# Attention and routing kernel: the row maxima turned by VectorE and sent by SyncE, a third unit loaded early, and a norm folded into the logits

## The reference, cut to what matters

```python
# x: (4, 1024, 256), fp32
x = x + _layernorm(attention(_layernorm(x)))
x = x + _layernorm(ffn(_layernorm(x)))

# attention: 16 heads of 16, relative positions (DeBERTa: content-to-position and position-to-content)
scores = einsum('bhqd,bhkd->bhqk', q, k) / scale
scores = scores + (c2p + p2c) / scale        # both gathered by the bucket of q - k
probs = softmax(scores)
out = layernorm((probs @ v) @ Wo + bo + hidden_states, 1e-7) * ln_scale + ln_bias

# ffn: router, then the one expert that it picks
routing_logits = x @ Wr + br                 # 8 experts, x is the normalised input
indices = argmax(softmax(routing_logits))
for i in range(8):
    h = relu((x * mask_i) @ W1[i] + b1[i]);  out = out + h @ W2[i] + b2[i]
```

## Time and profile before

| | us |
|---|---|
| median of 3 runs | 1785.49 |
| lowest, highest | 1784.4, 1792.77 |
| the profiled execution | 1794.4 |
| its span, first to last instruction | 1792.3 |

### The profile page before, as it was taken

How to read it: one execution, slowest core, us unless ns; L and a number is a source line. 1 busy time by engine, 2 the same in 40 slices (tenths; PEclk the granted TensorE clock), 3 DMA queues, 4 the chain that set the end, 5 groups by cost and what they waited for, 6 DMA issues and landing times. The chain is left out here.

```text
span 1792.3 us, 41887 instructions
## 1 busy us (share of the span) xinstructions
PE 1615.2 (90%) x13688; PEld 1147.8 (64%) x13688; DVE 1364.4 (76%) x3868; ACT 1145.8 (64%) x2764; POOL 1030.9 (58%) x1264
## 2 busy tenths in 40 slices
PE   7963799999999999999999999999977866999997
PEld 4531566666666666666666666666634646999996
DVE  4753798999998999898899998999956754555553
ACT  6852587877877888878777878787754631222221
POOL 0003776777776777777777777777814622333332
PEclk9985899999999999999999999999997857999998
DMA  4986788878888788788888887888608616666762
GB/s 136 332 284 221 246 278 275 273 264 267 269 280 275 261 275 279 256 272 286 269 265 267 268 274 260 273 264 281 211 25 220 190 65 197 194 193 198 206 202 57
DMA packets 292450, 421.65 MB, mean 235 GB/s; under 512 B 35382, under 2 KB 233804, under 8 KB 292139
## 3 DMA queue, kind: packets, MB, share of 16 engines
q1 hardware_dynamic: 271640, 378.99, 65.2%
q10 hardware_dynamic: 16851, 30.67, 5.6%
q0 software_dynamic: 3744, 9.31, 1.4%
HBM read 241.39 MB, written 177.79 MB: 234 GB/s over the span
## 5 line engine op out<-in xcount | busy, mean ns | idle before, releaser
L934 ACT ACTIVATE t_probsT<-t_flip 128x512 f32<-128x512 f32 x1024 | 603.2, 615 | 192.3 <-PE t_flip L791 103.3
L851 DVE TENSOR_REDUCE t_most<-t_scores 128x1 f32<-128x640 f32 (+1 forms) x512 | 435.7, 851 | 120.1 <-PE t_scores L775 119.4
L997 POOL TENSOR_TENSOR t_near<-t_near,masks 128x384 f32<-128x384 f32 (+1 forms) x128 | 146.5, 1144 | 275.5 <-DMA t_near<-skew_d 274.8
L861 DVE CUSTOM_DVE_ANT_0 t_band<-t_scores,t_near,t_most 128x384 f32<-128x384 f32 (+1 forms) x512 | 297.0, 580 | 0.5 <-DVE t_most L851 0.2
L872 DVE TENSOR_SCALAR_CACHE_REDUCE t_band<-t_band,t_top 128x384 f32<-128x384 f32 (+1 forms) x512 | 291.2, 569 | 0.0
L926 ACT COPY t_table<-t_table_ps 128x388 f32<-128x388 f32 x502 | 251.2, 500 | 54.1 <-PE t_table_ps L747 50.9
L812 PE MATMUL t_sum_ps<-t_probsT,vals 128*32 128x256 f32 x4096 | 274.3, 385 | 0.3 <-ACT t_probsT L934 0.3
L1013 POOL TENSOR_TENSOR t_near<-t_near,masks 128x768 f32<-128x768 f32 (+1 forms) x128 | 268.6, 2098 | 0.0
L775 PE MATMUL t_scores<-masks,t_near 128*128 128x128 f32 x1408 | 244.8, 278 | 19.6 <-POOLq L1016 18.8
L798 PE MATMUL t_flip<-masks,t_band 128*128 128x128 f32 x1408 | 258.1, 274 | 0.0
L768 PE MATMUL t_scores<-afters,quests 105*128 105x256 bf16 (+3 forms) x1024 | 244.3, 288 | 3.8 <-DVE t_top L861 3.6
(11 more groups left out here) (212 smaller groups left out, 2572.4 us busy)
## 6 DMA issues: line engine op xcount, KB each, us to landing
skew_d<-t_table SPq DMA_DIRECT2D x128, 1024.0 KB, 11.3
t_near<-skew_d SPq DMA_DIRECT2D x128, 640.0 KB, 8.0
t_near<-skew_d SPq DMA_DIRECT2D x128, 384.0 KB, 7.4
e_w<-in_L_ffn_W_dram ACTq DMA_DIRECT2D x39, 512.0 KB
e_w<-in_L_ffn_W_dram SPq DMA_DIRECT2D x39, 512.0 KB
split_d<-p_part SPq DMA_DIRECT2D x32, 384.0 KB, 3.3
afters<-split_d SPq DMA_DIRECT2D x128, 96.0 KB
quests<-split_d SPq DMA_DIRECT2D x128, 96.0 KB
```

Source lines behind the costliest of these rows:

```text
L851: nc.vector.tensor_reduce(most[:, c:c + 1], out[:, wide:S], AX.X, ALU.max).then_inc(far_seen, 1)
L861: nc.vector.tensor_tensor_reduce(band[n % 2][:, t, 0:wide], out[:, 0:wide], near[n % 2][:, 0, t, at:at + wide], 1.0, most[:, c:c + 1], ALU ...
L934: nc.scalar.activation(probsT[s % 4][:, half * 512:(half + 1) * 512], flip_ps[half][:, :], ACT.Exp, scale=SCALE).then_inc(expd, 1)
```

## The change

- `attend`, the maxima: the three parts lie in a tile of four (the fourth zero), VectorE turns them itself in four blocks of 32 by 32 (`turn_top`, after `look(s)` at s = 8n + 9), waiting for GpSimd's split. TensorE's L820 and ScalarE's L946 and L948 go, with the waits around them and the bf16 identity. SyncE issues the transfer (`send_top(u - 1)`), between the near read of unit u + 1 and the loads of unit u + 4.
- `attend`, loads: unit 2 is loaded in `project`, at its step 6 (`EARLY` = 3), the first `load_far` moves to step 7, and `Wo` is loaded at u = 12 into a tile kept for `mix`.
- `mix`: TensorE's program starts when `Wo` (landed long ago) and the bias rows are there. The third norm is not applied to the rows: their sum `x2` is turned and multiplied by `Wr` as it is, and the norm's factor and shift are put into the logits for all tokens at once behind the loop. ScalarE applies two norms instead of three in a step, and the loop of VectorE and ScalarE has 18 full steps instead of 20. The first two norms' statistics go to PSUM. `b1` is loaded by rows and turned by TensorE, not by a transfer of single elements.

```diff
-EARLY = 2
+EARLY = 3
@@ project, sync
                 if s == 6:
+                    hats.load_unit(sp, split_d, 2)
+                if s == 7:
                     hats.load_far(sp, far_d, 0)
@@ attend, sync
+            def send_top(n):
+                sp.wait_ge(top_turned, n + 1)
+                sp.dma_start(quest[n % BUFS][MROW:ROWS, :], topT[n % 2][0:PARTS * QT, :]).then_inc(top_in[n % BUFS], 16)
+
             for u in range(-2, N + 3):
...
                 if u == -2:
                     skew_read(0, 0)
+                if 0 <= u - 1 < N:
+                    send_top(u - 1)
                 if EARLY <= u + 4 < N:
                     load_unit(u + 4)
...
+                if u == 12:
+                    sp.dma_start(wo[:, :, :], Wo.rearrange("(k p) n -> p k n", p=P)).then_inc(wo_in, 16)
@@ attend, tensor
-                if x >= AHEAD and (x - AHEAD) % QT == 2:
-                    pe.wait_ge(top_kept, (x - AHEAD) // QT)
...
-            def turn_top(n):
-                pe.wait_ge(split_made, 5 * (n + 1))
-                pe.wait_ge(table_kept, by_act(min(n * QT + QT + AHEAD + 2, TS) - 1))
-                nc.tensor.matmul(table_ps[0:PARTS * QT, 0, 0:P],
-                                 top_part[n % 2][:, :, :].rearrange("p a t -> p (a t)"), ident16[:, :],
-                                 start=True, stop=True).then_inc(top_turned, 1)
@@ attend, vector
+            def turn_top(n):
+                dve.wait_ge(split_made, 5 * (n + 1))
+                if n < 2:
+                    dve.wait_ge(parts_set, 2)
+                if n >= 2:
+                    dve.wait_ge(top_in[(n - 2) % BUFS], 16 * ((n - 2) // BUFS + 1))
+                for a in range(4):
+                    last = nc.vector.transpose(topT[n % 2][:, 32 * a:32 * a + 32],
+                                               top_part[n % 2][32 * a:32 * a + 32, :, :].rearrange("p a t -> p (a t)"))
+                last.then_inc(top_turned, 1)
...
                 look(s)
+                if s > QT and s % QT == 1:
+                    turn_top(s // QT - 1)
@@ attend, scalar
-            def keep_top(n):
-                act.wait_ge(top_turned, n + 1)
...
-                nc.scalar.copy(topT[n % 2][:, :], table_ps[0:PARTS * QT, 0, 0:P]).then_inc(top_kept, 1)
-                act.wait_ge(top_kept, n + 1)
-                nc.scalar.dma_start(quest[n % BUFS][MROW:ROWS, :], topT[n % 2][:, :]).then_inc(top_in[n % BUFS], 16)
@@ mix, sync
-            loads = [(wo[:, :, :], Wo.rearrange("(k p) n -> p k n", p=P)),
-                     (ls_b[:, :], row(ln_s, D)), (lb_b[:, :], row(ln_b, D)),
+            loads = [(ls_b[:, :], row(ln_s, D)), (lb_b[:, :], row(ln_b, D)),
...
-            for dst, src in [(b1_sb[:, :, :], b1.rearrange("e (c p) -> p e c", p=P)), (b2_sb[:, :], b2),
+            for dst, src in [(b1_rows[:, :], b1.rearrange("e (c p) -> (e c) p", p=P)), (b2_sb[:, :], b2),
@@ mix, vector
+            dve.wait_ge(row_norm, 4)
             dve.wait_ge(logit_made, NG)
             link(nc.vector.tensor_tensor(logits[:, :, :], logit_ps[:, 0:NT * E].rearrange("p (t e) -> p t e", e=E),
-                                         br_b[:, :].unsqueeze(1).to_broadcast([P, NT, E]), ALU.add))
+                                         row_inv[:, :].unsqueeze(2).to_broadcast([P, NT, E]), ALU.mult))
+            link(nc.vector.tensor_tensor(logits[:, :, :], logits[:, :, :], offset[:, :, :], ALU.add))
@@ mix, scalar
-                for i in range(lo, hi):
+                for i in range(lo, min(hi, 2)):
@@ mix, tensor
-                pe.wait_ge(norm_made[2], g + 1)
+                pe.wait_ge(x2_made, g + 1)
-            pe.wait_ge(loaded, 16 * 6)
+            pe.wait_ge(wo_in, 16)
             pe.wait_ge(bo_made, 7)
```

More of the change, by code:

```diff
@@ L130, in build @@
             spent = sem.spend()
-            attend(nc, sem, spent, masks, rows, hats, split_d, far_d, v_d, skew_d, ctx_d)
+            attend(nc, sem, spent, masks, rows, hats, split_d, far_d, v_d, skew_d, ctx_d, Wo, wo, wo_in)
         sem.take_back(spent)
@@ L567, in _, with attend @@
                 last.then_inc(far_made, 1)
-def attend(nc, sem, spent, masks, rows, hats, split_d, far_d, v_d, skew_d, ctx_d):
+def attend(nc, sem, spent, masks, rows, hats, split_d, far_d, v_d, skew_d, ctx_d, Wo, wo, wo_in):
     AHEAD = 2 * QT + QT // 2
@@ L1037, in _ @@
             nc.gpsimd.memset(before_rows[:, :], -1.0).then_inc(before_set, 1)
+            for i in range(2):
+                nc.gpsimd.memset(top_part[i][:, PARTS:4, :], 0.0).then_inc(parts_set, 1)
             pool.wait_ge(before_set, 1)
@@ L1241, in _ @@
                 dve.wait_ge(stats_made, norms_before[s + 1])
-                for i in range(lo, hi):
+                if hi > 2:
+                    g = s - 2 * LAG
+                    for t in range(G):
+                        last = nc.vector.bn_aggr(row_mv[:, g * G + t, :], stats[:, c, 2, t, :])
+                    last.then_inc(row_mv_made, 1)
+                if s >= NORMED:
+                    continue
+                for i in range(lo, min(hi, 2)):
                     for t in range(G):
@@ L1346, in keep_xf @@
                 nc.scalar.copy(xfT[g % 2][:, :, :], xf_ps[:, :, :]).then_inc(xfT_made, 1)
-            for s in range(STEPS):
+            for s in range(NORMED):
                 if s in W2_AT:
@@ L1360, in _ @@
                 if hi > 1:
-                    a = max(lo, 1)
-                    last = nc.scalar.activation(root[:, c, a:hi, :], mv[:, c, a:hi, :, 1], ACT.Sqrt, bias=eps[:, 1:2])
+                    last = nc.scalar.activation(root[:, c, 1, :], mv[:, c, 1, :, 1], ACT.Sqrt, bias=eps[:, 1:2])
                 last.then_inc(root_made, 1)
-                if s >= 2 * LAG + 1:
-                    keep_xf(s - 2 * LAG - 1)
+                if s >= TURN:
+                    keep_xf(s - TURN)
                 act.wait_ge(shift_made, s + 1)
-                for i in range(lo, hi):
+                for i in range(lo, min(hi, 2)):
                     g = s - LAG * i
-                    src, dst = ((y1, y4), (y4, y5), (x2, xf))[i]
+                    src, dst = ((y1, y4), (y4, y5))[i]
                     if i == 1 and g >= BUFS:
                         act.wait_ge(x2_made, g - BUFS + 1)
-                    if i == 2 and g >= BUFS:
-                        act.wait_ge(xf_turned, g - BUFS + 1)
                     for t in range(G):
@@ L1377, in _ @@
                     last.then_inc(norm_made[i], 1)
-            keep_xf(NG - 1)
+            for g in range(NORMED - TURN, NG):
+                keep_xf(g)
+            act.wait_ge(row_mv_made, NG)
+            nc.scalar.activation(row_root[:, :], row_mv[:, :, 1], ACT.Sqrt, bias=eps[:, 1:2]).then_inc(row_root_made, 1)
             act.wait_ge(const_made, 2)
@@ L1428, in constant_rows @@
                 last.then_inc(const_made, 1)
[L1430 removed]
+            pe.wait_ge(wo_in, 16)
             pe.wait_ge(bo_made, 7)
             project_out(0)
[L1433 removed]
+            for s in range(NG + TURN + 1):
                 if s + 1 < NG:
                     project_out(s + 1)
[L1436 removed]
+                if s == 2:
+                    pe.wait_ge(loaded, 16 * 5)
+                    pe.wait_ge(const_in, 48)
+                    nc.tensor.transpose(aside_ps[:, 0:E * KC], b1_rows[:, :], ident[0:E * KC, 0:E * KC])
+                    for k in range(2):
+                        last = nc.tensor.matmul(aside_ps[:, E * KC:E * KC + E], masks[:, 3, :], wr[:, k, :],
+                                                start=(k == 0), stop=(k == 1))
+                    last.then_inc(aside_made, 1)
+                g = s - TURN
                 if 0 <= g < NG:
```

85 lines of the change are left out of this document (51 added, 34 removed).

## The result

| | us |
|---|---|
| before, median of 4 runs on the same chip | 1787.93 (1784.4 to 1792.77) |
| after, median of 4 runs | 1916.89 (1912.85 to 1919.51) |
| ratio | 1.072, 95% interval 1.068 to 1.0755 |
| predicted | 1820, range 1755 to 1880 |

The account below looks back on a forecast made before the run. The prediction took the queue of transfers to bound attention. From this execution's 1794.4 us, +61 for late maxima, -7 for the third unit and -20 for mix gave 1828.4, less 8.9 to the median: 1820 us, range 1755 to 1880.

Parts of the forecast that it names:

- The loop over two units: Attention: two periods = 20.4 + one unit's compute + 0.3 us, so period 18.8 against 17.8, +61 us.
- The queue drains: Attention: later flips mean later loads, so old work ahead goes; last flip to near read's landing falls from 23.7 to 20.4 us.
- rival 2: Attention: the maxima land in time despite the near read ahead of them, no stall; 1758 us, chance 0.20.
- a unit's compute without the queue: Attention: VectorE's 16.1 us, plus 0.4 for the transposes and 0.4 for waits that stay, 16.9 us.
- rival 1: Attention: stalls cost clock (1845 to 1880 us) or the queue doesn't drain (1936 us); chance 0.15.
- the spread in attention: Forecast's own spread from compute 16.5 to 17.3 and drained loop 19.6 to 21.2 us: +27 to +104 us.
- VectorE's turning: Attention: four small transposes a unit, 0.3 to 0.6 us, taken 0.4; ready at some 700.3, before the near read's issue.
- Rival 3: Attention: VectorE's transposes wait for GpSimd's split and hold up all looks; around 1840 us, chance 0.07.
- The queue is the bound: Attention: the queue of transfers sets the 17.8 us unit, though its mean share is 0.82; some engines must be full.
- Rival 4: Attention: compute, not the queue, is the bound and freed time counts; -30 to -55, 1704 to 1730 us, chance 0.08.
- Third unit early: Loading unit 2 in `project` lets table writes go 3 us earlier; gain 0 to 9 us, taken 7.
- `mix`: After attention: start -4, `b1` -2, steps -9, tail -5 us; sum -20, between -8 and -30.

Follow-up runs that it names:

- The filled stall: Changed kernel with 20 more products ahead of the first flip of every second unit, results overwritten: 1864.2 us, ratio 1.0439.
- with the queue relieved: Kernel before with all but the maxima's part, table writes cut to a quarter from unit 2 on (tells of time only): 1736.43 us, ratio 0.9694.
- the rest alone: Kernel before with early unit 2, early `Wo` and the whole of `mix`, maxima as before: 1766.55 us, ratio 0.988.
- the two with both places moved: Changed kernel, maxima turned one look sooner, issued by ScalarE (1769.47 us) or by SyncE ahead of the near read (1767.64 us).
- spread loads: Operand loads reordered, slowest dimension 16 rows, not three: all but the maxima 1761.55 us; changed kernel 1872.53; turned sooner with ScalarE issuing 1772.79.

## Why the prediction was wrong in size

**What held.** The maxima land right behind the near read. The loop over two units is the one that was written down: two periods = the way from the loads to the landing, one unit's compute, and 0.3 us. With the values of the trace after, (21.1 + 19.53 + 0.3)/2 = 20.5; the stalls come 40.8 us apart (202.68 to 1344.49 in 28 times), so 20.4. The queue drains as said: the way is 21.1 us (713.09 to 734.19), near the 20.4 taken, far from 23.7.

The Trainium skill's page DMA: Bandwidth & Descriptors, section on queues, rings and completion order, says that a queue is consumed in ring order and that queues take turns. The traces agree with both halves: on one queue the two landings release their engines 0.15 us apart, and from ScalarE's queue or from ahead of the read the maxima come in about 5 us (medians of the units that wait: 5.3 and 4.9). Its remark that completion isn't in order of issue, rival 2 of the prediction, brought nothing here.

**The step that failed** is the term "a unit's compute without the queue", 16.9 us. It was taken at full clock. In the stalled unit it is 19.53 us: +1.3 us a unit of the 1.7 missing; the longer way, +0.7, gives the other 0.35. The cause was on the page: the earlier trace rows show a clock of 0.57 for 4 us behind a gap in TensorE's work, and the prediction made of it rival 1, at 0.15, with 0.4 to 0.9 us a period. Its price was too low as well: it counted "a few us at half clock", 0.4 to 0.9 us a period, where the 6.8 us behind this stall lose 3.0 us in every second unit, so 1.5 us a period (1.4 by the median of the stalls). The filled stall shows that this is cause and not company. With the clock kept, the same formula gives (21.3 + 16.7 + 0.3)/2 = 19.15 us (21.3: the loads of a unit at 687.87 to the landing at some 709.2), and its two units of 38.4 us bear that out; the mean is 19.3. The filled kernel is still 44 us above the forecast: some 33 of them are 0.54 us a unit of period (0.45 by the longer way), and most of the rest is the 7 us of the third unit, whose gain the first stall eats there too (first exponential at 203.5 us).

Two of the prediction's sums don't come out as it gives them. From its own bounds the spread in attention is +24 to +98, not +27 to +104, and its other two terms together give 8 to 39 us back, not 16 to 39. Neither touches the forecast or its range.

**Size of the stall.** "Nearly 2 us a unit, perhaps 3 in every second one": it is 4.7, all in every second unit. The loop couples units two apart, so one can stand for both, and here one did throughout attention. Why the stall doesn't divide evenly was not tried.

**VectorE's turning** was put at 0.4 us a unit (it is 0.84) and on the path only through the near read's issue. The text noted that the maxima would be ready at 700.3 for 697.8 before and asked nothing more, since the read stood in front anyway. With the queue's order mended, its place, behind one look or two, is worth 60 us on ScalarE's queue (1830 to 1769) and 35 on SyncE's (1803 to 1768). It was neither a term nor a rival. Rival 3, VectorE waiting for the split, did not occur.

**What bounded the kernel.** "The queue is the bound" was half of it. The unit around the values' transfer lengthened, and 17.8 us was read from two units; other units of the same trace take 17.4, and with the queue relieved most units take that and none from 300 us on takes less than 17.3. Adding the VectorE busy time and an allowance for waits to 16.9 missed this. The 16.57 us of the unit that follows a stalled one isn't the steady rate either; what makes the difference of 0.8 us is open. Rival 4 (freed time on TensorE and ScalarE counts) fails: moving the turning to VectorE is worth nothing, 1769 and 1768 against 1767.

**The other terms.** Third unit early: 7 forecast, 5 by the first exponential; in the changed kernel the first stall, 7.5 us, eats it. `mix`: 20 forecast; 16.5 us with the rest alone and 19.7 in the changed kernel, less the 1 to 2 given back behind it, so 15 to 18 net. TensorE's wait at its start went from 13.61 to 9.50 us, now for the bias rows:

```profile
1488.82 2.04 PE L1430 MATMUL m_out_ps<-wo,m_heads 128*128 128x256 f32 x4 [9.50 <-DVE m_bo_part L1234]
```

and a full step takes 3.7 to 4.3 us, with GpSimd's three passes back to back, where 4.1 was forecast:

```profile
1511.59 1.28 POOL L1517 TENSOR_TENSOR m_y<-m_y,m_ls_b 128x512 f32<-128x512 f32 x1 [1.95 <-ACT m_y L1408]
...
1515.27 1.27 POOL L1517 TENSOR_TENSOR m_y<-m_y,m_ls_b 128x512 f32<-128x512 f32 x1
...
1519.55 1.27 POOL L1517 TENSOR_TENSOR m_y<-m_y,m_ls_b 128x512 f32<-128x512 f32 x1 [0.55 <-ACT m_y L1408]
```

The tail, from the last x2 (1574.98) to the logits (1580.87), is 5.9 us for 10.9: the 5 forecast.

**Better than both.** Five versions are 1.0 to 1.4% faster than the kernel before: the rest of the change alone, the two with both places moved, and spread loads with the first or with one of the others. The fastest median is that of the rest with spread loads (1761.55, ratio 0.9856 [0.9819, 0.9893]); these runs don't order the five among each other.

## What to carry to other kernels

A small transfer that an engine waits for is placed by its landing, not its issue: look what lies ahead of it on its own queue, and how old its data is when it is sent. Where a stall of several us repeats, price the engine's clock behind it as well as the stall: here filling the stall gave back 53 us of the 97 that the forecast lacked. And before a queue is called the bound, take the period of many units, not of two: the mean against the shortest units that repeat shows how much there is to gain. Beware of units that only catch up, as those of 16.57 us behind a stalled one.

## What was not expected of the hardware

Twenty useless products (4.5 us) in a stall of 4.7 us made the kernel 53 us faster, since the granted clock stayed at 1.00 where without them it was 0.56 in the mean of the next 6.8 us. And cutting a load along 16 rows and not three took the table writes behind it from 11.1 to 8.0 us of landing time, at the same period. The Trainium skill, page DMA: Bandwidth & Descriptors, section on why a DMA increments its semaphore by 16, says that a transfer is shared by the largest number of engines, up to 16, that divides the slowest dimension on both of its sides. The shorter landings agree with it, but no run here shows single engines.
